# Six edits to a four-layer attention and FFN kernel: two score buffers in the layer-3 attention, and five smaller moves and rewrites

## The reference, cut to what matters

```python
rh = gelu(attn_out @ res_inter_w + res_inter_b)
res_mlp_out = rh @ res_output_w + res_output_b
out = res_mlp_out * coef[:, :1] + moe_out * coef[:, 1:] + residual
```

```python
amax = clip(max(abs(x)), 1e-8)          # over all tokens
x_sim = clip(round(x * 32767 / amax), -32768, 32767) * amax / 32767
hidden = gelu(x_sim @ W_in_sim + b_in)
out = quantize_a16(hidden) @ W_out_sim + b_out
```

## Time and profile before

| | us |
|---|---|
| median of 3 runs (lowest, highest) | 3071.56 (3067.39, 3076.02) |
| the profiled execution's own time | 3070.32 |
| its span, first to last instruction | 3068.8 |
| busy: PE, DVE, ACT, POOL | 2563.7, 2210.2, 1393.5, 385.9 |
| mean granted TensorE clock | 0.927 |

### The profile page before, as it was taken

One profiled execution on the slowest core, in us unless ns is written; L12 is line 12 of the kernel. 1 busy time (PEld: TensorE's weight loads), 2 busy tenths in 40 slices (PEclk: granted clock), 3 DMA queues, 4 the chain that ended last, 5 costly groups with the idle time before them and its releaser, 6 DMA issues. The chain is left out here.

```text
span 3068.8 us, 68519 instructions
## 1 busy us (share of the span) xinstructions
PE 2563.7 (84%) x25419; PEld 1890.9 (62%) x25454; DVE 2210.2 (72%) x5434; ACT 1393.5 (45%) x2483; POOL 385.9 (13%) x542
## 2 busy tenths in 40 slices
PE   4867769995899999999999789887979786787457
PEld 3644436663887877878876466665657454666227
DVE  6889859996567767777775388896830486888784
ACT  3548868884011111111111477764534345666364
POOL 0012210000000000000000000002321442232004
PEclk9988779997999999999999799998989898999689
DMA  3110000002113112112120000001013220000001
GB/s 92 31 67 1 0 19 16 14 13 91 76 56 111 56 61 106 56 67 99 56 80 31 21 15 15 10 2 36 26 36 110 79 66 3 0 0 0 8 0 55
DMA packets 55450, 128.94 MB, mean 42 GB/s; under 512 B 9702, under 2 KB 21350, under 8 KB 54507
## 3 DMA queue, kind: packets, MB, share of 16 engines
q1 hardware_dynamic: 47754, 106.36, 10.0%
q0 software_dynamic: 7520, 20.34, 2.2%
HBM read 109.37 MB, written 17.30 MB: 41 GB/s over the span
## 5 line engine op out<-in xcount | busy, mean ns | idle before, releaser
L1505 PE MATMUL banks<-l1f_feed,l1f_w 128*128 128x512 f32 x512 | 229.1, 598 | 1.4 <-DVE l1f_feed L1774 1.4
L1448 PE MATMUL banks<-l1f_sums,l1f_mixes 128*128 128x256 f32 x768 | 186.6, 379 | 0.0
L1774 DVE TENSOR_TENSOR l1f_feed<-l1f_aoT,l1f_rwb 128x512 f32<-128x512 f32 x256 | 158.8, 682 | 15.8 <-PE banks L1448 10.3
L1505 PEld LDWEIGHTS banks<-l1f_feed,l1f_w 128*128 128x128 f32 x512 | 95.8, 192 | 108.5 <-issue 90.0
L1448 PEld LDWEIGHTS banks<-l1f_sums,l1f_mixes 128*128 128x128 f32 x768 | 145.9, 190 | 19.9
L1448 PE MATMUL banks<-l1f_feed,l1f_mixes 128*128 128x256 f32 x512 | 135.3, 387 | 20.5 <-DVE l1f_feed L1731 20.5
L1740 DVE TENSOR_TENSOR l1f_sums<-l1f_feed 128x512 f32<-128x512 f32 x128 | 88.5, 691 | 87.8 <-PE banks L1448 84.0
L1468 PE MATMUL banks<-l1f_w,l1f_feed 128*128 128x128 f32 x1024 | 136.7, 277 | 0.0
L214 POOL COPY x<-xn 128x512 f32 (+1 forms) x16 | 9.8, 611 | 935.6 <-DVE xn L1791 935.6
L1468 PEld LDWEIGHTS banks<-l1f_w,l1f_feed 128*128 128x128 f32 x1024 | 126.2, 194 | 0.0
L1448 PEld LDWEIGHTS banks<-l1f_feed,l1f_mixes 128*128 128x128 f32 x512 | 93.1, 192 | 38.7 <-DVE l1f_feed L1731 24.5
(11 more groups left out here) (524 smaller groups left out, 7057.5 us busy)
## 6 DMA issues: line engine op xcount, KB each, us to landing
l1f_rwb<-l1f_shares SPq DMA_DIRECT2D x128, 512.0 KB, 7.0
l0a_ctxT<-in_ctxT SPq DMA_DIRECT2D x16, 256.0 KB, 2.6
l2f_sent<-l0f_zero SPq DMA_DIRECT2D x4, 1024.0 KB, 7.0
l1a_ctxT<-in_ctxT SPq DMA_DIRECT2D x16, 256.0 KB, 2.6
l2c_ctxT<-in_ctxT SPq DMA_DIRECT2D x16, 256.0 KB, 2.7
l2e_rows<-l2f_sent SPq DMA_DIRECT2D x16, 256.0 KB, 2.8
l2f_answers<-l2e_y POOLq DMA_DIRECT2D x16, 256.0 KB, 2.7
l3p_ctxT<-in_ctxT SPq DMA_DIRECT2D x16, 256.0 KB, 2.6
```

Of the source, the lines that this page charges most:

```text
L1448: return pe.matmul(prods[:, n, :], left, right, start=(p == 0 and first), stop=(p == PAIRS - 1), skip_group_check=True)
L1505: pe.matmul(out_bank, w[:, 1, e, :], feed[:, e % NB, :], start=(e == 0), stop=(e == E - 1)).then_inc(s.y_psum, 1)
L1774: dve.tensor_tensor(feed[:, e % NB, :], aoT[:, m, :], rwb[:, m, e, :], ALU.mult).then_inc(s.ae_ready, 1)
```

## The change

1. Layer-0 attention: TensorE's keys go from the fourth to the first place of its list.
2. Layer-3 attention: the scores lie in two pairs of banks, 64 rows and 512 columns per product; `kbd` is twice as wide and made ahead of the mask row; score waits for the centring two tiles back; transposes, copies, weighing and what follows come one tile later against the scores, with four probability buffers; and the scores themselves come one round later against the preparations.
3. Layer-2 gate: the down bias is split by VectorE into three bf16 rows and added by one bf16 product of 96 rows.
4. The layer-3 network's weights are loaded and rounded in the expert stage, in buffers that live from there on.
5. Scales: for 40 of the 64 tiles ScalarE makes the absolute distance from the mean, and VectorE takes one maximum of it; for the other 24 the two reductions stay.
6. Up: the turned W_in and h stay fp32, one product for each bank; `low` is gone.

```diff
-            pipeline(pe, k.NG, [(1, turn), (2, outer), (3, project), (1, keys), (1, queries), (2, weigh), (1, values), (2, turn_o)])
+            pipeline(pe, k.NG, [(1, keys), (1, turn), (2, outer), (3, project), (1, queries), (2, weigh), (1, values), (2, turn_o)])
...
-        kbd = sb("kbd", [P, 2, 2, 4, S])
+        kbd = sb("kbd", [P, 2, H // 2, P])
...
-        top = sb("top", [P, 16])
-        prob = sb("prob", [P, 2, 16, S])
+        top = sb("top", [P, 2, H])
+        prob = sb("prob", [P, TG, H, S])
...
-        scores = k.banks[:, 0:4, 0:4 * S].rearrange("p a (b n) -> p a b n", n=S)
+        scores = [k.banks[:, 2 * par:2 * par + 2, :].rearrange("p a (h n) -> p (a h) n", n=S) for par in range(2)]
...
-                if mask:
-                    mask.make(pool, t, par, s.score_psum)
                 wait(pool, s.score_psum, t - 1)
                 settle(pool, k)
-                pool.tensor_tensor(kbd[:, par],
-                                   r.kT[:, bass.ds(P * t, P)].rearrange("p (b n) -> p b n", b=2).unsqueeze(2).to_broadcast([P, 2, 4, S]),
-                                   k.headmask.unsqueeze(1).unsqueeze(3).to_broadcast([P, 2, 4, S]), ALU.mult).then_inc(s.q_ready, 1)
+                pool.tensor_tensor(kbd[:, par], r.kT[:, bass.ds(P * t, P)].unsqueeze(1).to_broadcast([P, H // 2, P]),
+                                   k.headmask8.unsqueeze(2).to_broadcast([P, H // 2, P]), ALU.mult).then_inc(s.q_ready, 1)
+                mask.make(pool, t, par, s.score_psum)
...
-            pipeline(pool, k.NT, [(5, copy_mv), (2, add_bias), (0, prepare)], unroll=TG)
+            pipeline(pool, k.NT, [(7, copy_mv), (2, add_bias), (0, prepare)], unroll=TG)
...
-                wait(pe, s.centred, t)
...
+                wait(pe, s.centred, t - 1)
+                rhs = mask.rhs(pe, t, par)
+                for a in range(2):
+                    pe.matmul(ps[2 * par + a], never[:, :], rhs, start=True, stop=False, skip_group_check=True)
+                for a in range(2):
+                    rows = slice(64 * a, 64 * a + 64)
                     for b in range(2):
...
+                        keys = slice(S * b, S * b + S)
+                        last = pe.matmul(ps[2 * par + a][keys, :], qT[rows, par, keys], kbd[rows, par, :, keys], start=False, stop=True,
...
-            pipeline(pe, k.NT, [(1, score), (2, turn), (4, project), (3, weigh)], unroll=TG)
+            pipeline(pe, k.NT, [(2, score), (4, turn), (6, project), (5, weigh)], unroll=TG)
...
-            pipeline(act, k.NT, [(0, copy_q), (2, copy_v), (2, copy_pT), (1, exp)], unroll=TG)
+            pipeline(act, k.NT, [(0, copy_q), (4, copy_v), (4, copy_pT), (2, exp)], unroll=TG)
...
-                wait(dve, s.pT_psum, t - 1)
...
+                wait(dve, s.pT_psum, t - TG + 1)
+                dve.tensor_tensor(prob[:, j], scores[par], top[:, par].unsqueeze(2).to_broadcast([P, H, S]), ALU.subtract)\
...
-            pipeline(dve, k.NT, [(1, centre), (3, normalise), (4, new_x)], unroll=TG)
+            pipeline(dve, k.NT, [(2, centre), (5, normalise), (6, new_x)], unroll=TG)
...
             finish_stats_act(act, k, s)
...
+            for t in range(FAR):
+                last = act.activation(away[:, t, :], k.x[:, OWN + t, :], ACT.Abs, bias=k.mv[:, OWN + t, 0:1], scale=-1.0)
+                if t % PIECE == PIECE - 1:
+                    last.then_inc(s.away_ready, 1)
...
+            for n in range(FAR // PIECE):
+                piece = slice(PIECE * n, PIECE * n + PIECE)
+                dve.wait_ge(s.away_ready, n + 1)
+                dve.tensor_reduce(far[:, piece], away[:, piece, :], AX_X, ALU.max).then_inc(s.ends_chain, 1)
...
                 for c in range(FC):
                     wait(pe, s.f_ready, FC * (g - 1) + c + 1)
-                    pe.matmul(ps[4 + c], w.win[:, c, :], high[:, m, :], start=True, stop=False)
-                    pe.matmul(ps[4 + c], w.win[:, c, :], low[:, m, :], start=False, stop=True).then_inc(s.f_psum, 1)
+                    pe.matmul(ps[4 + c], w.win[:, c, :], hT[:, m, :], start=True, stop=True).then_inc(s.f_psum, 1)
...
-            pipeline(dve, k.NG, [(1, lower), (0, quantise), (2, largest)])
+            pipeline(dve, k.NG, [(0, quantise), (2, largest)])
...
-                pe.matmul(y_bank, k.ones[0:1, 0:P], b2[:, :], start=True, stop=False, skip_group_check=True)
+                pe.matmul(y_bank, ones[0:96, :], b2_rows[:, :].unsqueeze(1).to_broadcast([96, TG, D]), start=True, stop=False,
+                          skip_group_check=True)
...
             dve.wait_ge(s.weights, 16 * 7)
+            chain.did(dve.memset(b2_rows[:, :], 0.0))
+            go(dve.tensor_copy(b2_part[:, 0, :], b2[:, :]))
...
+                last = dve.tensor_copy(b2_rows[32 * n:32 * n + 1, :], b2_part[32 * n:32 * n + 1, n, :])
+            last.then_inc(s.consts_ready, 1)
...
+            for dst, name in ((network.in_T, "L3_ffn_W_inT"), (network.wout, "L3_ffn_W_out")):
+                sp.dma_start(dst[:, :, :].rearrange("p a b -> p (a b)"), d[name]).then_inc(s.network_loaded, 16)
...
             pipeline(sp, items, [(0, load)], unroll=2 * per)
...
             pipeline(pe, items, [(1, up), (0, turn), (2, down)], unroll=2 * per, behind=2 * per)
+            pe.wait_ge(s.win_ready, 1)
+            for c in range(FC):
+                last = pe.transpose(ps[1][:, P * c:P * c + P], network.in_T[:, c, :], k.ident)
...
+            round_network()
             pipeline(dve, items, [(2, bias)], unroll=2 * per)
```

More of the change, by code:

```diff
@@ L2376, in _ @@
             dve.tensor_scalar(k.rstd[:, :], k.mv[:, :, 1], LN_EPS, None, ALU.add).then_inc(s.var_ready, 1)
-            for n in range(PIECES):
-                piece = slice(TP * n, TP * n + TP)
-                dve.tensor_reduce(ends[:, 0, piece], k.x[:, piece, :], AX_X, ALU.max).then_inc(s.ends_chain, 1)
-                dve.tensor_reduce(ends[:, 1, piece], k.x[:, piece, :], AX_X, ALU.min).then_inc(s.ends_chain, 1)
+            dve.tensor_reduce(ends[:, 0, :], k.x[:, 0:OWN, :], AX_X, ALU.max).then_inc(s.ends_chain, 1)
@@ L2387, in _ @@
-            dve.wait_ge(s.rstd_ready, 1)
-            dve.tensor_tensor(ends[:, :, :], ends[:, :, :], both(k.rstd[:, :]), ALU.mult).then_inc(s.ends_chain, 1)
-            dve.wait_ge(s.ends_chain, 2 * PIECES + 2)
-            dve.tensor_reduce(w.most[:, 0:1], ends[:, :, :].rearrange("p a t -> p (a t)"), AX_X, ALU.max,
-                              apply_absolute_value=True).then_inc(s.most_ready, 1)
-            chain = Chain(dve, s.w_chain)
-            go = lambda ins: chain.wait(chain.did(ins))
@@ new lines, in _ @@
+            dve.wait_ge(s.ends_chain, 3 + FAR // PIECE)
+            dve.wait_ge(s.rstd_ready, 1)
+            dve.tensor_tensor(peaks[:, 0:2 * OWN].rearrange("p (a t) -> p a t", a=2), ends[:, :, :], both(k.rstd[:, 0:OWN]), ALU.mult)\
+                .then_inc(s.ends_chain, 1)
+            dve.tensor_tensor(peaks[:, 2 * OWN:], far[:, :], k.rstd[:, OWN:], ALU.mult).then_inc(s.ends_chain, 1)
+            dve.wait_ge(s.ends_chain, 5 + FAR // PIECE)
+            dve.tensor_reduce(w.most[:, 0:1], peaks[:, :], AX_X, ALU.max, apply_absolute_value=True).then_inc(s.most_ready, 1)
@@ L2415, in l3_ffn_up @@
+def l3_ffn_up(nc, k, w, hidden):
     FC = F0 // P
@@ L2448, in _, with copy_hT @@
             act.wait_ge(s.scale_ready, 1)
-            def split(g, m):
+            def copy_hT(g, m):
                 act.wait_ge(s.hT_psum, g + 1)
                 wait(act, s.f_psum, FC * (g - 1))
-                act.copy(high[:, m, :], ps[m]).then_inc(s.high_ready, 1)
+                act.copy(hT[:, m, :], ps[m]).then_inc(s.hT_ready, 1)
             def gelu(g, m):
@@ L2547, in levels @@
                 settle(act, k)
-                act.activation(f[:, m], w.hidden[:, :, bass.ds(GT * g, GT)], ACT.Identity, bias=half_up[:, 0:1],
+                act.activation(f[:, m], hidden[:, :, bass.ds(GT * g, GT)], ACT.Identity, bias=half_up[:, 0:1],
                                scale=w.most[:, 1:2]).then_inc(s.rounded, 1)
@@ L2598, in phase_l2_ffn @@
         l2_ffn_gate(nc, k, w)
-        l2_ffn_experts(nc, k, w)
+        l2_ffn_experts(nc, k, w, network)
 def l2_ffn_gate(nc, k, w):
@@ L2952, in _ @@
             pipeline(act, items, [(1, gelu), (0, scale)], unroll=2 * per)
+            act.wait_ge(s.win_psum, 1)
+            act.copy(network.win[:, :, :].rearrange("p a b -> p (a b)"), ps[1])
         @block.vector
```

164 lines of the change are left out of this document (77 added, 87 removed).

## The result

| | before | after |
|---|---|---|
| median (lowest, highest), us | 3071.25 (3067.39, 3076.02), 4 runs | 3005.15 (3000.70, 3010.72), 4 runs |
| the profiled execution's own time, its span | 3070.3, 3068.8 | 3000.7, 2999.1 |
| mean granted TensorE clock | 0.927 | 0.941 |

The ratio of the times is 0.9785, 95% interval 0.9771 to 0.9799: 66 us less. The forecast was 3014, with a range of 2999 to 3036.

The account below looks back on a forecast made before the run. No single engine bounds the barrier-separated stages, so each edit was costed in its own stage. Terms -15 - 10 - 4 - 3 + 3 - 28 = -57 took 3070.3 to 3013, 3014 us on the median's footing; range 2999 to 3036.

Parts of the forecast that it names:

- 16.8 per four: Layer-3 attention: VectorE as the bound takes 3 x (4.05 - 0.38) + 5.81 = 16.8 us per four tiles.
- the 3.67 and the 5.81: Layer-3 attention: VectorE's plain round, 4.05 less 0.38 idle, and its 5.81 us round that also updates x.
- no idle before its reduction: Layer-3 attention, sign of being right: VectorE has no idle before its reduction, with score tiles about 4.2 us apart.
- the 95% forecast: Layer-3 attention, sign of being right: VectorE over 95% busy between score tiles.
- The +2 "at the lower clock at the start, where little is gained": Layer-3 attention start: wider scores cost twice as much at the lower clock and first score waits 0.4 more; +2 us.
- D, the slower case: Layer-3 attention at 1.2 GHz: TensorE needs 7.8 us per tile, up to 3014 + 230; chance 0.03.
- Rival B: Layer 0 gains nothing because features are late or VectorE fills the gap: 3029 us; chance 0.1.
- The +2 of the expert stage: Expert stage: four more loads issued by SyncE and half a megabyte ahead of the first rows, +2 us, not hidden.
- The 5.05: Up stage: new fp32 loop of copy 0.59, products 3.6, last GELU 0.70, handovers 0.15, in us per group.
- the 5.27 of before: Up stage: the old loop's time per group in us, against which the new loop gains 0.2 x 13 = 2.6.
- 5.4 for two groups: Up stage start: two fp32 groups at the lower clock take 8.6 us each against about 5.9, +5.4 us.
- Rival C: Up stage's fp32 products at 1.2 GHz throughout: 47 us more, 3061; chance of over +10 is 0.08.

Follow-up runs that it names:

- the table of the two halves: Changed kernel with two or one score buffers, transposes late or early: two/late 3005.15 us, two/early 3017.47, one/late 3039.89, one/early 3038.66.
- the keys-only trace: Kernel before with only layer 0's keys put first: median 3057.7 us, on before 0.9951; the traced second run took 3051.93 us.

## Why the prediction was right, and where it was off

**Layer-3 attention, -28 forecast, -31.4 measured.** The mechanism was right: the single score buffer set the pace, and the table of the two halves shows it. The size came out of three parts, of which one was costed. Between the first and the last reduction, behind the first four tiles, 275.9 us became 248.1: -27.8. Some 7 of the 275.9 were drops of the clock that are gone after, and which the forecast's 4.68 us per tile held too, unnamed. The forecast had 30 for all tiles, with 16.8 per four. That 16.8 was near 16.90 by two errors that cancel: VectorE's own rounds are 3 x 3.56 + 5.62 = 16.3, not 16.8, because the 3.67 and the 5.81 were read from rounds next to a wait, and the same steps take 3.56 and 5.62 in the kernel after; and two of the four rounds are 0.3 longer, one by waiting for the scores. So the sign "no idle before its reduction" did not come: 17 of the 64 reductions still wait, the 0.20 of each group among them, and VectorE is busy for 208.86 of 220 us, just under the 95% forecast. Not foreseen was the filling: with nothing to normalise yet and two buffers, the first tiles follow one another by 2.4 us, and the first four take 11.85 instead of 19.26: -7.4. A part of this is the clock and not the buffers. Before, it rose to 2.4 GHz 14 us behind the first reduction, after, with it (2579.0 and 2536.4 in the two traces); in the keys-only trace, with the attention of before, it rose 7 us behind it, and the first four tiles take 17.2. Not foreseen either was the price of the deeper lags at the end: from the last reduction to the next stage 17.5 us instead of 14.6, +2.9; and the first reduction comes 0.9 later. The +2 "at the lower clock at the start, where little is gained" is the step that failed: the start gained most per tile, and it was not left at the lower clock.

**The four probability buffers**, said to keep the subtraction from waiting: true for 0.15 us per four tiles only. **The later transposes**, meant to take the exponential out of TensorE's queue: right, 12 us, but only together with the second score buffer.

**GpSimd's doubled product** was put at 2.1 and takes 1.90; TensorE's mask waited for it twice, 3.7 us in all. D, the slower case, did not come: the clock of the attention rose from 0.91 to 0.98.

**Layer 0, -15 forecast, -14.5 measured.** By the working of the prediction the round went from 8.85 to (163.7 - 0.6 - 46.9) / 15 = 7.75, forecast 7.8: -16.5 over 15 rounds. Against it the first masked product is 2.0 us later (46.9, before 44.9), because in the first rounds the keys now stand ahead of the first turn and nothing waits for ScalarE there; they also take longer at first (8 products in 1.91 us, later 1.05). The prediction left this out; its count of 14 rounds covered it by chance. The engine named as next was wrong too: the 7.8 was to be held by VectorE, with an estimated 7.4 and a wait, and it is held by TensorE, 88.38 us busy of 90. Rival B is out.

**Gate, -10 forecast, -12.1 measured.** The round shown went from 10.01 to 9.19, near the 0.83 worked out. But others are shorter, as an early one (bias products at 2095.14 and 2104.12) with 8.98: from the first bias product to the last, 15 rounds, 145.9 us became 132.7, 0.88 each, so a little more than the bias product went; what, the runs don't tell. The splitting cost 2.35 ahead of the first group (the first normalisation comes 7.95 behind the start of the stage, before 5.6), not 1.6. The mis-sized term is the number of rounds and what one gives: -13.2 over these 15, where 0.83 over 14 = 11.6 was taken. The first bias product comes 1.1 later by the splitting, and that leaves the 12.1.

**Network moved and scales split, -6 and -3 (-9) forecast in the scales stage, -10.2 measured.** Neither was tried alone, but the two traces part them: from the start of the stage to the end of its last reduction 19.0 us became 15.1, -3.9 for the split, and from there to the next stage 7.6 became 1.3, -6.3 for the rounding. The 0.31 us per absolute distance, taken from the GELU rows, is 0.29; ScalarE does end last, as worked out. The +2 of the expert stage is +1.6. The runs with the loads on ScalarE show where it comes from: TensorE's first rows come 3.8 and 4.0 us behind the start of the stage with them, 5.1 to 5.9 in the seven kernels with the loads on SyncE, and 2.8 to 2.9 in the kernels without the loads. The lengths of the stage fit, but touch: 136.4 and 137.9 us against 137.9 to 142.9 in the seven.

**Up, +3 forecast, +1.9 measured in the two traces, +3.4 against its own undoing.** The sign was right and the parts were not. The loop was said to gain 0.2 per group; at the upper level of the clock it loses 0.35 (5.28 against 4.93). Two steps of the sum are off. The 5.05 put the handovers too low: the round from the copy at 2852.23 to the next at 2857.53 is 0.72 until the products start, 3.70 for them, and 0.88 until the next copy. And the 5.27 of before was a mean over two clock levels, set against a fp32 round at the upper one alone. The low clock was said to cost 5.4 for two groups; it caught only one, 6.34 instead of 3.70, and from the first copy to the second that is 1.3 more than before. The other rounds cost 1.1 more, and the end 0.5 less: +1.9. Rival C did not come: behind its first group the fp32 stage kept the upper level.

**Stages without an edit**, costed at nothing, gave -4.9; 2 of it in the layer-0 FFN. The same code moves by 4 us from one kernel's trace to another's in the gate stage and by 8 in the last stage, so no cause is claimed. The sum of the touched stages is -64.7, the forecast -57: of the difference, 3.4 are the attention, 2.1 the gate, 1.2 the scales, 1.1 the up stage. By the medians the change came out at -66, 9 below the forecast of 3014 and inside its range.

## What to carry to other kernels

When a loop that goes through a buffer is found, cost its filling and its draining apart from its steady pace: here the steady pace gave 27.8 us, the filling 7.4, and the drain took back 2.9. Look at the clock of both kernels beside them: part of the first two numbers was a clock that rose earlier and no longer dropped. Test a pair of edits as a two by two table: the later transposes were worth 12 us with two score buffers and nothing with one, which no undoing of single edits alone would tell. And compare an engine's round at equal clock, and take it from the steady part of a loop: 5.27 us as a mean over two levels was 4.93 at the upper one, and the loop that replaced it takes 5.28.

## What the runs showed of the hardware that was not expected

- VectorE's steps with an SBUF source and target (128 columns, fp32) took 1.83 us for four beside GpSimd's small casts and differences, 1.10 without. The Trainium skill (SBUF — State Buffer, "SBUF: two separate sides") says that such steps in a fast mode and GpSimd lock one another out for a whole instruction; the row agrees in kind: VectorE's four steps stretch by 0.7. That they ran in such a mode, no row shows. In the attention, where VectorE's maxima and subtraction read PSUM, they kept 1.22 and 1.23 us beside a GpSimd product of 1.90.
- GpSimd's product by a mask took 1.04 us at 512 columns and 1.90 at 1024: a little less than double.
- VectorE's next reduction follows the start of the 0.29 us multiplication by 0.21 us in most rounds without a wait, in the kernel before (2699.82 and 2700.03) as in the one after (2721.24 and 2721.45), and by 0.29 in the 3.85 round after.
- The clock stayed at 2.4 GHz in the attention after from 2570 to 2790, with TensorE busy for 206.63 of 220 us. Before, with 200.45 of 250 from 2600 on, it fell for a moment about every eight tiles. One fall is this row of the kernel before, and the round around it, from 2694.86 to 2700.03, takes 5.17 instead of 4.15:

```profile
2695.00:2698.00 3.00, 3.00 (x42) 2.74 (x40) 2.31 (x2) 1.84 (x4) 1.37 (x2) 0.50 0.00 0
```
